# Message stage of a graph network: the turning of edge codes and of the hidden rows rebuilt

## The reference, cut to what matters

```
Hb  = einsum('ni,bio->bno', h, V)               # 4 bases
m   = sum_b w_comp[etype][:, b] * Hb[b][src]    # a message per edge
agg = segment_sum(m * norm, dst)
hn  = relu(agg + h @ loop_w + bias)
y   = hn @ ffn_w.T + ffn_b + h
y   = layernorm(y) * ln_g + ln_b                # eps 1e-8
x   = layernorm(x + y)
```

## Time and profile before

| | |
|---|---|
| Median of three executions | 2154.86 us (2153.06 to 2154.87) |
| The profiled execution | 2157.03 us, its span 2155.0 us |
| TensorE matmul busy | 2070.5 us, 96% of the span |
| VectorE, ScalarE, GpSimd busy | 1521.9, 1269.1, 663.1 us |
| Message stage | up to about 1126 us of the span, 25 tiles |
| Granted TensorE clock | 0.993 of full speed, mean |

### The profile page before, as it was taken

How to read it: one execution, slowest core, us unless ns; L and a number is a source line. 1 busy time by engine, 2 the same in 40 slices (tenths; PEclk the granted TensorE clock), 3 DMA queues, 4 the chain that set the end, 5 groups by cost and what they waited for, 6 DMA issues and landing times. The chain is left out here.

```text
span 2155.0 us, 53971 instructions
## 1 busy us (share of the span) xinstructions
PE 2070.5 (96%) x19640; PEld 1668.4 (77%) x19640; DVE 1521.9 (71%) x4217; ACT 1269.1 (59%) x2225; POOL 663.1 (31%) x802
## 2 busy tenths in 40 slices
PE   1899999999999999999989999999998999999998
PEld 1788888888888888888865777777775677777776
DVE  3777888788788878878736666666664667667665
ACT  0466666666666666666644555665553566555664
POOL 2656566566556656655300000000000000000000
PEclk9999999999999999999999999999999999999999
DMA  3011111111111111111112222222111222222220
GB/s 79 6 46 52 49 37 60 50 37 47 52 49 47 51 50 37 47 52 47 42 66 108 91 70 80 89 89 89 64 55 62 95 97 96 96 75 86 95 96 8
DMA packets 43152, 137.12 MB, mean 64 GB/s; under 512 B 9195, under 2 KB 24489, under 8 KB 36614
## 3 DMA queue, kind: packets, MB, share of 16 engines
q1 hardware_dynamic: 38614, 128.31, 16.6%
q0 software_dynamic: 4400, 6.80, 1.3%
HBM read 91.89 MB, written 43.20 MB: 63 GB/s over the span
## 5 line engine op out<-in xcount | busy, mean ns | idle before, releaser
L848 PE MATMUL ps<-matrixT,x_rows 125*128 125x256 f32 (+1 forms) x2500 | 581.1, 383 | 1.7 <-ACT aggT L940 1.7
L921 ACT COPY matrixT<-ps 125x500 f32<-125x500 f32 (+2 forms) x800 | 395.8, 584 | 245.5 <-PE ps L836 242.2
L848 PEld LDWEIGHTS ps<-matrixT,x_rows 125*128 125x128 f32 x2500 | 459.6, 190 | 69.3 <-issue 2.2
L1550 ACT COPY weightsT_l<-ps 125x500 f32<-125x500 f32 (+1 forms) x450 | 233.8, 542 | 369.4 <-PE ps L1471 369.4
L1628 DVE CUSTOM_DVE_ANT_0 scores_l<-ps,bias_rows_l 125x500 f32<-125x500 f32 (+1 forms) x700 | 396.8, 619 | 42.4 <-issue 41.2
L836 PE MATMUL ps<-high_weights,low_onehot 64*125 64x125 f32 x6300 | 404.6, 279 | 11.9 <-ACT matrixT L921 8.8
L836 PEld LDWEIGHTS ps<-high_weights,low_onehot 64*125 64x125 f32 x6300 | 366.7, 189 | 46.2 <-issue 29.6
L1471 PEld LDWEIGHTS ps<-eye,scores_l 125*125 125x125 f32 x2500 | 301.0, 189 | 115.6 <-issue 97.3
L1471 PE MATMUL ps<-eye,scores_l 125*125 125x125 f32 x2500 | 364.1, 286 | 4.7 <-ACT scores_l L1532 3.4
L1636 DVE COPY weightsT_l<-ps 125x500 f32<-125x500 f32 (+1 forms) x250 | 150.0, 600 | 268.2 <-PE ps L1471 265.9
L1532 ACT ACTIVATE scores_l<-scores_l,neg_max_l 125x1500 f32<-125x1500 f32 x200 | 320.9, 1605 | 20.2 <-DVE neg_max_l L1665 20.2
(11 more groups left out here) (153 smaller groups left out, 1614.9 us busy)
## 6 DMA issues: line engine op xcount, KB each, us to landing
bias_rows_l<-bias SPq DMA_DIRECT2D x50, 1562.5 KB, 6.6
bias<-bias SPq DMA_DIRECT2D x75, 500.0 KB, 2.6
x_rows<-in_x SPq DMA_DIRECT2D x1, 1562.5 KB
bias<-bias SPq DMA_DIRECT2D x25, 62.5 KB, 1.6
x<-x_rows SPq DMA_DIRECT2D x25, 62.5 KB
x_rows_l<-x SPq DMA_DIRECT2D x25, 62.5 KB
out<-rows_l SPq DMA_DIRECT2D x25, 62.5 KB
dst_int<-in_dst SPq DMA_DIRECT2D x1, 402.8 KB
```

The source lines that it names most:

```text
L848: last = nc.tensor.matmul(psG[:, BASES * SPLIT * side:BASES * (SPLIT * side + SIDE[side])], x[:, h, :], MT[side][:, 0:SIDE[side], BASES * ...
L921: last = nc.scalar.copy(MT[side][:, at:at + 2 * c - 1:2, 0:COLS], psP[bank][0:R, :].rearrange("p (i c) -> p i c", c=128)[:, 0:c, 0:COLS])
L1550: nc.scalar.copy(PT[i % 8][:, 0:cw[c]], psT[i % 2][0:R, 0:cw[c]]).then_inc(z["pa_ok"], 1)
```

## The change

- The planes of base weights are stored twice, side by side (`codes`: base, copy, slot). One transpose of a 128x128 array in float32 turns a base for both halves of the partitions: 4 transposes into bank 6.
- The two digit planes become a tile of their own, `digits`, in bf16 and doubled in the same way, and two bf16 transposes turn them into columns 128 to 255 of bank 7 (`psD`). OWN goes from 512 to 128, so that bf16 holds every value.
- Since even nodes go to one half of the partitions and odd nodes to the other, ScalarE picks columns with a step of two, and the two copies become four, each of 64 partitions.
- VectorE's last two operations of `slot_kinds` and GpSimd's and VectorE's last one of each base write twice as many elements.
- The product of the hidden rows is formed with `loop_w` and `V` stationary and `xt` and `aggT` moving, so that it comes out with the features as partitions. VectorE's maximum and TensorE's transpose go, and ScalarE applies bias and relu in one operation, in k=5 ahead of the period's evacuation, not in k=6.
- TensorE waits in `turn_codes` for `h_ok` of the tile before, and ahead of the ffn product of k=6 for `codesT_ok`, since bank 7 now holds the digits too.
- The tile `loop_bias_rows` and its load go.

```diff
+        digits = [sb(f"digits{i}", [128, 2, 2, SLOTS], BF16) for i in range(2)]
-        codes = [sb(f"codes{i}", [128, PLANES, SLOTS], F32) for i in range(2)]
+        codes = [sb(f"codes{i}", [128, BASES, 2, SLOTS], F32) for i in range(2)]
...
-                    last = nc.gpsimd.tensor_tensor(to[:, 2 + b, :], part[:, 0, :], part[:, 1, :], ALU.add)
+                    last = nc.gpsimd.tensor_tensor(to[:, b, :, :], twice(part[:, 0, :]), twice(part[:, 1, :]), ALU.add)
...
-                V.tensor_copy(to[:, 1, :], chunk[:, :])
-                V.tensor_tensor(to[:, 0, :], low[:, :], off[:, :], ALU.add).then_inc(kinds_ok, 1)
+                V.tensor_copy(to[:, 1, :, :], twice(chunk[:, :]))
+                V.tensor_tensor(to[:, 0, :, :], twice(low[:, :]), twice(off[:, :]), ALU.add).then_inc(kinds_ok, 1)
...
-                    if k == 5 and inside(u):
-                        relu(u)
...
-                for c in range(PLANES):
-                    for q in range(2):
-                        last = nc.tensor.matmul(psK[SLOTS * q:SLOTS * (q + 1), SLOTS * c:SLOTS * c + PAIRS], codes[par][:, c, :],
-                                                eye[:, q:2 * PAIRS:2], start=True, stop=True)
+                for b in range(BASES):
+                    nc.tensor.transpose(psK[:, 128 * b:128 * (b + 1)], codes[par][:, b, :, :].rearrange("p q n -> p (q n)"), eye[:, :])
+                if s >= 2 if is_int(s) else True:
+                    pe.wait_ge(h_ok, s - 1)
+                for c in range(2):
+                    last = nc.tensor.transpose(psD[:, c, :], digits[par][:, c, :, :].rearrange("p q n -> p (q n)"), eye16[:, :])
...
-                        acc = psM[0:R, 0:D]
-                        nc.tensor.matmul(acc, xt[:, :], loopw[:, :], start=True, stop=False)
+                        acc = psM[:, 0:R]
+                        nc.tensor.matmul(acc, loopw[:, :], xt[:, :], start=True, stop=False)
                         for b in range(BASES):
-                            last = nc.tensor.matmul(acc, aggT[:, b, :], V_b[:, b, :], start=False, stop=(b == BASES - 1))
+                            last = nc.tensor.matmul(acc, V_b[:, b, :], aggT[:, b, :], start=False, stop=(b == BASES - 1))
...
-                    if k == 5 and inside(u):
-                        pe.wait_ge(hrow_ok, u + 1)
-                        nc.tensor.transpose(psM[:, 128:128 + R], hrow[:, :], eye[0:R, 0:R]).then_inc(h_ps, 1)
...
                     if k == 6 and inside(u):
                         pe.wait_ge(h_ok, u + 1)
+                        if inside(w + 1):
+                            pe.wait_ge(codesT_ok, w + 2)
...
-                    if k == 6 and inside(u):
-                        act.wait_ge(h_ps, u + 1)
+                    if k == 5 and inside(u):
+                        act.wait_ge(m_ps, u + 1)
...
-                        nc.scalar.activation(hT[:, :], psM[:, 128:128 + R], ACT.Identity, bias=lcol[:, :]).then_inc(h_ok, 1)
+                        nc.scalar.activation(hT[:, :], psM[:, 0:R], ACT.Relu, bias=lcol[:, :]).then_inc(h_ok, 1)
...
-                        nc.scalar.copy(digitsT[par][:, :, :], turned[:, 0:2, 0:PAIRS])
-                        nc.scalar.copy(weightsT[par][:, :, :],
-                                       turned[:, 2:PLANES, 0:PAIRS].rearrange("p c n -> p n c")).then_inc(codesT_ok, 1)
+                        turned = psK[:, :].rearrange("p (b n) -> p n b", n=128)
+                        for q in range(2):
+                            own, pick = slice(SLOTS * q, SLOTS * (q + 1)), slice(q, q + 2 * PAIRS - 1, 2)
+                            nc.scalar.copy(digitsT[par][own, :, :], psD[own, :, pick])
+                            last = nc.scalar.copy(weightsT[par][own, :, :], turned[own, pick, :])
+                        last.then_inc(codesT_ok, 1)
```

More of the change, by code:

```diff
@@ L34 @@
 ROWS_PER = EC // ROW
-PLANES = 2 + BASES
 COLS = (BASES + 1) * T
@@ L45 @@
 EARLY, FIRST_ON_V = 2, 3
-OWN = 512.0
+OWN = 128.0
 BLOCKS = -(-EDGES // 128)
@@ L133, in build @@
                 m["ids"] = sb1("ids", [128, T], F32)
-                m["loop_bias_rows"], m["loop_bias_col"] = sb1("loop_bias_rows", [R, D], F32), sb1("loop_bias_col", [D, 1], F32)
+                m["loop_bias_col"] = sb1("loop_bias_col", [D, 1], F32)
                 m["ffn_b_rows"] = sb1("ffn_b_rows", [R, D], F32)
@@ L173, in load_weights @@
     load(m["ffn_b"][:, :], a["L0_gnn_ffn_b"].rearrange("(a n) -> a n", a=1))
-    load(m["loop_bias_rows"][:, :], a["L0_gnn_bias"].partition_broadcast(R))
     load(m["loop_bias_col"][:, :], a["L0_gnn_bias"].rearrange("(n a) -> n a", a=1))
@@ L185, in load_weights @@
         load(m[f"bs{layer}"][:, :], a[f"L1_gnn_bs{layer}"].partition_broadcast(R))
-W_IN = 16 * (10 + 2 * 8)
+W_IN = 16 * (9 + 2 * 8)
 TURNS = [(g, min(4, T - g)) for g in range(0, T, 4)]
@@ L509, in message @@
         held = sb("held", [128, 1], F32)
-        hrow = sb("m_h_rows", [R, D], F32)
         hT = sb("m_hT", [D, R], F32)
@@ L515, in message @@
         raised = [sb(f"x_raised{i}", [R, D], F32) for i in range(2)]
-        lneg = sb("loop_bias_neg", [R, D], F32)
         xnew = [sb(f"x1_rows{i}", [R, D], F32) for i in range(2)]
@@ L524, in message @@
         psM = ps[7]
+        psD = psM[:, 128:256].bitcast(BF16).rearrange("p (c n) -> p c n", n=128)
         psC = psT[:, :].bitcast(BF16).rearrange("p (h n) -> p h n", n=128)
         (const, s2, slot_ok, gps, codes_ok, codes_ps, codesT_ok, hot, built, pairs_ok, evac_ok, agg_ok, aggT_ok,
-         ctA_ok, ctB_ok, c_ps, ln_ok, bias_ok, xt_ok, m_ps, hrow_ok, h_ps, h_ok, y_ps, y_ok, x_ok, x_ps, x_t_ok, asked1, rooted1,
-         asked2, rooted2, nrm1, nrm2, lifted, s3, kinds_ok, lneg_ok, blank_ok, turned_ps, turned_ok, first_v, first_ok) = (
+         ctA_ok, ctB_ok, c_ps, ln_ok, bias_ok, xt_ok, m_ps, h_ok, y_ps, y_ok, x_ok, x_ps, x_t_ok, asked1, rooted1,
+         asked2, rooted2, nrm1, nrm2, lifted, s3, kinds_ok, blank_ok, turned_ps, turned_ok, first_v, first_ok) = (
             sem("m_" + n) for n in (
@@ L531, in message @@
                 "pairs_ok", "evac_ok", "agg_ok", "aggT_ok", "ctA_ok", "ctB_ok", "c_ps", "ln_ok", "bias_ok", "xt_ok", "m_ps",
-                "hrow_ok", "h_ps", "h_ok", "y_ps", "y_ok", "x_ok", "x_ps", "x_t_ok", "asked1", "rooted1", "asked2", "rooted2",
-                "norms1", "norms2", "lifted", "s3", "kinds_ok", "lneg_ok", "blank_ok", "turned_ps", "turned_ok",
+                "h_ok", "y_ps", "y_ok", "x_ok", "x_ps", "x_t_ok", "asked1", "rooted1", "asked2", "rooted2",
+                "norms1", "norms2", "lifted", "s3", "kinds_ok", "blank_ok", "turned_ps", "turned_ok",
                 "first_v", "first_ok"))
@@ L540, in message, with twice @@
         block = ctx.enter_context(nc.Block())
+        def twice(t):
+            return t.unsqueeze(1).to_broadcast([128, 2, SLOTS])
         def size(k):
@@ L670, in slot_kinds @@
                 then = Steps(v, s3, s * 4)
-                to = codes[par]
+                to = digits[par]
                 v.wait_ge(ell_in[par], (half(s, par) + 1) * 64)
@@ L697, in first_coefs @@
                     then(V.tensor_tensor(part_v[:, 0:2, :], part_v[:, 0:2, :], part_v[:, 2:4, :], ALU.add))
-                    last = V.tensor_tensor(to[:, 2 + b, :], part_v[:, 0, :], part_v[:, 1, :], ALU.add)
+                    last = V.tensor_tensor(to[:, b, :, :], twice(part_v[:, 0, :]), twice(part_v[:, 1, :]), ALU.add)
                     if b < BASES - 1:
@@ L741, in moments @@
                 return V.tensor_scalar_add(roots[which][par][:, :], means[which][par][:, 1:2], eps)
[L743 to L751, removed]
             def first(u, par):
@@ L979, in step @@
                             act.wait_ge(built, w * PERIODS)
-                        turned = psK[:, 0:PLANES * SLOTS].rearrange("p (c n) -> p c n", n=SLOTS)
-                        nc.scalar.copy(digitsT[par][:, :, :], turned[:, 0:2, 0:PAIRS])
-                        nc.scalar.copy(weightsT[par][:, :, :],
-                                       turned[:, 2:PLANES, 0:PAIRS].rearrange("p c n -> p n c")).then_inc(codesT_ok, 1)
+                        turned = psK[:, :].rearrange("p (b n) -> p n b", n=128)
[4 more added lines that the diff above has]
+                        last.then_inc(codesT_ok, 1)
                     if k == 6 and is_int(w) and w == 0:
```

## The result

The changed kernel takes 2146.21 us in the median of six executions (2142.84 to 2147.18) against 2154.86 before (2153.06 to 2158.24 in six): the ratio is 0.9957, 95% interval 0.9945 to 0.997, so 0.3% to 0.55% faster. The forecast was 2145.3, 0.9 us lower. The profiled execution took 2147.18 us with a span of 2144.7, against 2157.03 and 2155.0. Of the executions of the experiments, two of the kernel before and one of `e9_twice_counts_later` ran at a granted clock of 0.75 to 0.85 and took 2383 to 2620 us; no ratio counts them.

What follows compares the result with a forecast made beforehand. TensorE's instructions end to end were taken to bound the kernel. 24 x 0.42 = 10.1 us saved, less 0.5 at the start, gives -9.6 and a median of 2145.3 us; 8-in-10 range 2141.0 to 2151.5.

Steps and rivals of the forecast that it cites:

- TensorE is the bound: Steady tile: TensorE is busy for the whole 41.87 us, so other engines count only if they come late.
- The block of six transposes: Turning of the codes: four float32 transposes at 0.11 us and two bf16 take 0.65 us against 0.86.
- Rival A: Turning of the codes: float32 transposes cost 0.17 us each, like the lone one; 2151.0 us; chance 0.09.
- Rival B: Turning of the codes: float32 transposes run at one pass like bf16, 0.057 us; 2140.3 us; chance 0.09.
- L893 at 0.21 us: Period 5: the lone transpose of the hidden rows goes altogether, saving 0.21 us a tile.
- The product of the hidden rows: TensorE's ten instructions with sides swapped: change taken as 0, +-0.6 us over the run, staying at 1.18 us.
- The steady sum: 24 turnings and 24 removed transposes in the full stream: 24 x 0.42 = 10.1 us gained.
- Cost 0: ScalarE: four copies take 0.84 us, leaving 0.65 us before TensorE wants the evacuation for period 7.
- Rival C: ScalarE comes late at period 7 if copies exceed 1.49 us; at 2.3 us, 2164.8 us; chance 0.04.
- VectorE and GpSimd: Doubled writes add at most 0.3 us each and 4.6 us a tile, covered by slack; cost 0.
- The first tile: Start chain: VectorE +0.4, ScalarE +0.42, TensorE -0.3; together +0.5 us once.
- The last tile: The ffn product follows a count transpose waiting for the logarithm, and the removed transpose sat idle; gain 0.

Runs made afterwards that it cites:

- e9_twice_counts_later: Changed kernel with ScalarE's four copies made twice and the first piece of the counts moved behind period 6's evacuation; 2146.04 us, ratio 0.9955.
- e3: Changed kernel with each of the four float32 transposes made twice into the same place; 2156.8 us, ratio 1.0009.
- e5: Changed kernel with the base weights in bf16 too, so all six transposes are bf16; 2140.44 us, ratio 0.9934.
- e2: Kernel before with the new turning of the codes but the old hidden rows; 2148.58 us, ratio 0.9968.
- e1: Changed kernel with the old turning of the codes, keeping the new hidden rows; 2152.27 us, ratio 0.9985.
- e6: Changed kernel with the moving side of the hidden rows' product padded from 125 to 128 columns; 2145.03 us in one execution.
- e0: The changed kernel itself, unaltered, run again beside the others; 2145.39 us, ratio 0.9955.
- e7: Changed kernel with both digit copies first, then both weight copies; 2148.82 us in one execution.
- e4: Changed kernel with ScalarE's four copies made a second time, into tiles nobody reads; 2168.14 us, ratio 1.006.

## Why the prediction was right, point by point

**TensorE is the bound.** Right. e3 adds 0.108 us of time for every added transpose, and a tile's window is full of TensorE's work before and after.

**The block of six transposes.** Forecast 0.65 us, measured 0.65. The 0.11 us for a float32 one is right to the hundredth. Of the five rows that it was taken from, the early 128-wide transposes, scaled (0.117), and the float32 products (0.108) came nearest. Rival A, priced by a lone transpose right behind a switch of the array's split, is out: such a row holds more than the transpose's pace. Rival B is what bf16 does, by e5, and float32 doesn't. The rule of the Trainium skill (TensorE: Matmul & The Clock Gate, Terms) that the transpose mode is 4 times faster for float32 is not borne out here. A float32 product of this size is two instructions 0.108 us apart, so 0.216 us, and the float32 transpose takes 0.11, half of it and not a quarter; a bf16 transpose takes 0.055.

**L893 at 0.21 us.** The sum is right and the reading was not quite. e2 shows that the transpose is 0.12 us of this and the switch from the full array to the column-split codes 0.09; e1 shows that the switch stays if only the transpose goes. The change takes out the transpose and the column-split products together, and so the forecast could not go wrong on it. That is luck as far as this reading goes: for either half alone the same reading fails. It gives 4.3 us for e1, with the dearer product already counted, where 2.2 came, and 5.0 for e2 where 7.4 came.

**The product of the hidden rows.** Taken at 0, within 0.025 us to either side. It cost 0.03 a tile, 0.7 us in all, and e6 rules out the moving side as the cause. This is the term of the steady sum that was off. The 0.9 us between forecast and median can't be put down to it, since medians of this very kernel differ by as much: e0 has 2145.39, 0.1 from the forecast.

**The steady sum.** 24 x (0.42 - 0.03) = 9.4 us; the inner stretch gives 9.49.

**ScalarE.** "Cost 0" held, but with less to spare than was claimed. Forecast were 0.84 us for the copies and a slack of 0.65; measured were 1.07 us and 0.18 that can be used. The 0.47 us between the slacks are three parts. The copies took 0.23 more: that four would follow each other at the old pace is the step that failed, since copies on changing partitions don't overlap (e7). The counts took 1.11 us ahead of the evacuation, where the 1.01 was read ahead of L965, 0.10 more. And 0.14 lie between the evacuation's end and the products that wait for it, which the forecast had at nothing (e4). The price beyond the slack was rightly put at 2.4 us for every 0.1 us: e4 has 21.3 us for 0.89. Rival C, the slower one, is the mechanism that e4 shows; it begins at 1.25 us of copies and not at 1.49.

**VectorE and GpSimd.** GpSimd's last operation went from 740 to 880 ns, VectorE's two from 196 and 219 to 226 and 283 ns, all far from doubling. Neither TensorE nor ScalarE waited for them between 300 and 900 us; GpSimd waits for VectorE's codes about as long as before, 4.2 us a tile for 4.1.

**The first tile.** +0.5 us was forecast. The first products start at 52.81 us and before at 52.70. The chain's own parts: from the start of the turning to the first products 4.91 us for 4.64 before, 0.27 more. Forecast was 0.42 for ScalarE less 0.3 for TensorE there. TensorE's turning is 0.25 us shorter (48.06 to 49.70 before, 47.90 to 49.29 now), and the rest is ScalarE's, 0.52 more. The further 0.4 forecast for VectorE does not show: the turning starts at 47.90 and not later than before. By the second turning, 87.89 against 87.91, nothing of the +0.5 is seen, though the start of that one moves by more than 3 us between executions, so that neither value is proven.

**The last tile.** No gain there, as forecast: TensorE's ffn product comes at once after the count transpose that waits for the logarithm.

```profile
1110.73 0.24 PE L852 MATMUL ps<-eye,countsT 125*125 125x125 bf16 x1 [1.28 <-ACT ln L938]
1110.81 0.44 PE L888 MATMUL ps<-ffnT,m_hT 128*125 128x128 f32 x2
```

From that transpose to the second stage's first product it is 1118.72 - 1110.73 = 7.99 us, and was 1128.23 - 1120.24 = 7.99.

## What to carry to other kernels

Where one engine is busy without a gap, price an edit by the distances from start to start in its timeline, and keep the price of a switch of the array's split apart from that of the instruction that happens to stand before it: it moves to the neighbour, and goes only when the split itself goes. Once such an engine gets faster, look which buffer it will ask for next; here 0.18 us of slack on an engine busy 60% were left, and moving one operation behind the one that was waited for made room for 1.07 us more. Slack read up to the end of a record is too large by what lies between that end and the start of the waiting instruction, 0.14 us here. Measure a small steady gain between two marks inside the profile where the total scatters by half of it.

## What the runs showed that was not expected

ScalarE overlaps a digit copy with the weight copy on the same partitions by 0.1 us (0.25 us long, 0.15 from start to start). It does not overlap any of these copies with a next one that begins on other partitions: 0.37 us from start to start for a copy of 0.36, and in e7 0.26 for digit copies of 0.25. The same partitions are not enough for an overlap, though: the counts and the evacuation behind them both begin on partition 0, and stand 1.11 us apart for 1.08. What decides there, no run shows.

The difference between the profiled executions of the changed kernel comes almost all from the first tile. There TensorE works in bursts with waits of 2.2 us between them, and how fast a burst runs differs from one to the other. Two windows of bursts of the changed kernel, 32 instructions each, the second and the fifth, in its own profile:

```profile
58.75:62.40 3.65, 3.65 (x32) 3.44 (x32) 3.58 (x8) 0.00 (x0) 3.34 (x5) 1.00 0.00 0
75.55:79.10 3.55, 3.55 (x32) 3.43 (x32) 3.55 (x5) 0.00 (x0) 3.16 (x5) 0.50 0.00 0
```

and the second burst in the profile of e0_after:

```profile
58.53:60.50 1.97, 1.97 (x32) 1.82 (x32) 1.97 (x2) 0.00 (x0) 1.81 (x3) 1.00 0.00 0
```

The granted clock in the row at 75.55 is 0.50, the 1.2 GHz level, and the burst takes 3.55 us. At 58.53 it is 1.00, 2.4 GHz, and it takes 1.97. The row at 58.75 says 1.00 and yet takes 3.65 us. That 1.00 is not a reading: the trace's first record of the clock stands at 68.00 us in this execution and at 56.95 in e0_after, and a window without a record prints 1.00. The duration is what tells, and by it the second burst ran at the lower level here and at the higher in e0_after. Why the two executions differ, no run shows. By the second tile's turning one was 3.5 us ahead of the other (84.36 against 87.89), which is what their spans differ by, 2140.8 against 2144.7, all but 0.4 us.
